# Cross-attention with neighbour features on one core: low-byte loads issued from ACT's queue, projection evicted by ACT and masked by POOL, layer statistics one step later

## The reference

```
for layer in (L0, L1):            # x -> x
    x = norm(attn(ctx, ctx, ctx) + x)   # per channel over tokens
x = x + neighbour_sum(ctx, x)     # L2
x = norm(attn(ctx, ctx, ctx) + x) # L3

attn: q, k, v = W_in @ ctx + b_in; 8 heads of 16, chunks of 64 tokens
      p = softmax(q k^T / 4 + (0 if mask > 0 else -1e9)); o = p v
      out = (W_out @ o + b_out) * mask
neighbour_sum: for each token its 30 nearest by channels 0..2 of ctx (top_k of
      -|p_i - p_j|^2); spherical features of the differences (rho, theta, phi);
      three 1x1 layers with batch norm over all batches; softmax over the 30;
      weighted sum of x at the neighbours
```

## Time and profile before

| what | us |
|---|---|
| three runs | 6677.32, 6666.21, 6669.81 |
| median | 6669.81 |
| the profiled execution: its time, its span | 6667.89, 6665.9 |
| busy in the span: PE, DVE, ACT, POOL | 5685.7, 5886.1, 4461.5, 3249.3 |
| mean granted clock of PE in the span | 0.904 of full |

### The profile page before, as it was taken

One profiled execution on the slowest core, in us unless ns is written; L12 is line 12 of the kernel. 1 busy time (PEld: TensorE's weight loads), 2 busy tenths in 40 slices (PEclk: granted clock), 3 DMA queues, 4 the chain that ended last, 5 costly groups with the idle time before them and its releaser, 6 DMA issues. The chain is left out here.

```text
span 6665.9 us, 228315 instructions
## 1 busy us (share of the span) xinstructions
PE 5685.7 (85%) x83284; PEld 3456.0 (52%) x83284; DVE 5886.1 (88%) x8332; ACT 4461.5 (67%) x17049; POOL 3249.3 (49%) x3279
## 2 busy tenths in 40 slices
PE   7888888888888888888888888888839949999998
PEld 3454545455555545545554555555423337677776
DVE  7999999999999999999999999999946588777776
ACT  7787878787787878787877878788822533333333
POOL 3455655555555555555655555555550023333332
PEclk9999988898888999898898998998859979999999
DMA  2333333233333333333233333333241013333332
GB/s 48 89 97 85 93 91 91 84 91 87 100 92 91 97 85 94 91 90 91 85 92 102 91 91 92 93 91 90 80 118 35 0 38 90 90 83 89 87 84 78
DMA packets 633780, 564.50 MB, mean 85 GB/s; under 512 B 535517, under 2 KB 557277, under 8 KB 598653
## 3 DMA queue, kind: packets, MB, share of 16 engines
q1 hardware_dynamic: 632572, 548.75, 29.1%
HBM read 380.55 MB, written 67.24 MB: 67 GB/s over the span
## 5 line engine op out<-in xcount | busy, mean ns | idle before, releaser
L703 ACT ACTIVATE prob<-SC,row_max 128x64 f32<-128x64 f32 x6144 | 1835.3, 327 | 671.7 <-DVE row_max L1032 664.8
L817 POOL TENSOR_TENSOR prob<-prob,row_rec 128x512 f32<-128x512 f32 x768 | 829.9, 1081 | 1897.7 <-DVE row_rec L1040 1897.1
L703 ACT ACTIVATION_READ_ACCUMULATOR prob<-SC,row_max 128x1 f32 x6144 | 1349.0, 220 | 0.0
L1024 DVE FIND_INDEX8 nbr<-top,dist 128x8 uint16<-128x1024 f32 x1024 | 1235.8, 1220 | 0.0
L1017 DVE MAX8 top<-dist 128x8 f32<-128x1024 f32 x1024 | 1194.1, 1207 | 12.6 <-DVE y_b L1055 10.3
L610 PE MATMUL PT<-ident,prob 128*128 128x128 f32 x3072 | 516.1, 295 | 573.9 <-ACT prob_t L710 563.2
L610 PEld LDWEIGHTS PT<-ident,prob 128*128 128x128 f32 x3072 | 383.6, 151 | 1076.8 <-issue 1033.2
L589 PE MATMUL SC<-k_bd,q_t 128*64 128x256 f32 x6144 | 935.8, 430 | 0.0
L1019 DVE MATCH_REPLACE8 dist<-top,dist 128x1024 f32<-128x1024 f32 x768 | 925.2, 1210 | 0.0
L1816 DVE TENSOR_TENSOR d_oh_a<-lo,iota_a 128x4096 bf16<-128x4096 bf16 x256 | 584.4, 2293 | 255.2 <-PE DM L1667 254.8
L1708 ACT ACTIVATE dense<-DM 128x512 f32<-128x512 f32 x512 | 305.6, 597 | 746.3 <-PE DM L1667 746.1
(11 more groups left out here) (194 smaller groups left out, 9538.6 us busy)
## 6 DMA issues: line engine op xcount, KB each, us to landing
low_all<-low_scratch SPq DMA_DIRECT2D x256, 1024.0 KB, 4.9
k_bd<-k_t SPq DMA_DIRECT2D x3072, 16.0 KB, 1.9
placed<-compact SPq DMA_DIRECT2D x256, 192.0 KB, 3.7
ctx<-in_ctx SPq DMA_DIRECT2D x32, 512.0 KB, 4.0
mask<-in_mask SPq DMA_DIRECT2D x32, 512.0 KB, 7.8
xb<-in_x SPq DMA_DIRECT2D x32, 512.0 KB, 4.3
x_scratch<-xb SPq DMA_DIRECT2D x32, 512.0 KB, 4.7
y_scratch<-y_b SPq DMA_DIRECT2D x32, 512.0 KB, 6.6
```

Of the source, the lines that this page charges most:

```text
L703: last = act.activation(prob[:, s % 4, g * CHUNK:(g + 1) * CHUNK], SC[:, s % 2, g * CHUNK:(g + 1) * CHUNK], ACT.Exp, bias=row_max[:, s % 2 ...
L817: pool.tensor_tensor(pr, pr, row_rec[:, r % 2, :].unsqueeze(2).to_broadcast([128, 8, CHUNK]), ALU.mult).then_inc(normed, 1)
L1024: last = dve.max_index(nbr[:, uu % BPB, t, k * 8:(k + 1) * 8], best, row)
```

## The change

1. LAG_BN and LAG_LN are one step larger: 8 and 9.
2. load_low moves from SP to ACT. ACT issues it at the end of its step, behind the exponentials and the copies of that step; tile 0 in step 24 + 6, tile 1 in step 24 + 8, tile t + 2 in step 24 + 12 + 3t. It waits for the stores of the low part (before SP waited for them once) and for the fetch as before.
3. The y bank is evicted by ACT with the bias added, in the same step, behind the other projections of that step and ahead of the copy to dist and the exponentials; ACT also takes over the three waits that guard y_b.
4. POOL multiplies y_b with the mask in place, for all three layers, once ACT has freed the bank, and signals y_masked; its addition of x waits for that. SP's store of the third layer waits for y_masked instead of masked, and for mask_row_ready ahead of the next mask load.

```diff
-LAG_BN, LAG_LN, LAG_TOP = 7, 8, 2
+LAG_BN, LAG_LN, LAG_TOP = 8, 9, 2
...
@@ sync, step
-                v = lagging(i, s, LOW_IN_AT)
-                if v is not None:
-                    sp.wait_ge(low_out, START + (i * BPB + v + 1) * 64)
-                    alone(sp)
-                    for t in range(2):
-                        load_low(i, v, t)
                 v = lagging(i, s, 6)
                 if v is not None:
                     b = i * BPB + v
-                    sp.wait_ge(masked, START + b + 1)
+                    sp.wait_ge(y_masked, START + (b + 1) * 2 * LAYERS)
+                    alone(sp)
+                    sp.wait_ge(mask_row_ready, START + b + 1)
...
-                at = lagging_tile(i, s, SELECT_AT)
-                if at is not None and at[1] + 2 < NT:
-                    load_low(i, at[0], at[1] + 2)
@@ scalar
+            def load_low(i, v, t):
+                tile = (i * BPB + v) * NT + t
+                act.wait_ge(low_out, START + (i * BPB + v + 1) * 64)
+                act.wait_ge(fetched, at_least(i, START + 2 * (tile - 1), START))
+                alone(act)
+                act.dma_start(low_all[:, t % 2, :], dram["low"][i * BPB + v][t:t + 1].broadcast_to([128, GROUPS * 128])).then_inc(low_in[t % 2], 16)
@@ scalar, step, behind the projections
+                r = s - LAG_Y
+                if real(i, r, STEPS) and r % 4 == 3:
+                    jj, uu = place(r)
+                    h = (r % PAIRS) // 4
+                    bank, free = produced(i, ("y", r // PAIRS, h))
+                    if h == 0:
+                        if jj == 0:
+                            act.wait_ge(applied[1], START + i * BPB + uu)
+                        elif jj == 1:
+                            act.wait_ge(y3_out, START + (i * BPB + uu) * 16)
+                        else:
+                            act.wait_ge(applied[0], START + i * BPB + uu + 1)
+                    act.activation(y_b[:, y_half(r // PAIRS), h * HALF:(h + 1) * HALF], bank, ACT.Identity, bias=b_out[:, jj:jj + 1]).then_inc(free, 1)
@@ scalar, step, behind the copy to picked
+                for t in range(2):
+                    v = lagging(i, s, LOW_IN_AT + 2 * t)
+                    if v is not None:
+                        load_low(i, v, t)
+                at = lagging_tile(i, s, SELECT_AT)
+                if at is not None and at[1] + 2 < NT:
+                    load_low(i, at[0], at[1] + 2)
@@ gpsimd, step
-                if real(i, r, STEPS) and r % 4 == 3 and place(r)[0] < 2:
+                if real(i, r, STEPS) and r % 4 == 3:
                     jj, uu = place(r)
                     h = (r % PAIRS) // 4
+                    half = slice(h * HALF, (h + 1) * HALF)
+                    mine = y_b[:, y_half(r // PAIRS), half]
                     copied(pool, i, ("y", r // PAIRS, h))
-                    half = slice(h * HALF, (h + 1) * HALF)
+                    landed(pool, mask_in, i, uu)
+                    pool.tensor_tensor(mine, mine, mask[:, uu % BPB, half], ALU.mult).then_inc(y_masked, 1)
+                if real(i, r, STEPS) and r % 4 == 3 and place(r)[0] < 2:
...
+                    pool.wait_ge(y_masked, START + (i * BPB + uu) * 2 * LAYERS + 2 * jj + h + 1)
@@ vector, step
-                r = s - LAG_Y
-                if real(i, r, STEPS) and r % 4 == 3:
...
-                    dve.wait_ge(pj_ready, START + use_count(i, use, 1))
...
-                    dve.scalar_tensor_tensor(y_b[:, y_half(r // PAIRS), half], PJ[:, use_parity(i, use), :], b_out[:, jj:jj + 1], mask[:, uu % BPB, half],
-                                             ALU.add, ALU.mult).then_inc(pj_free[use_parity(i, use)], 1)
...
```

More of the change, by code:

```diff
@@ L266, in attention_and_neighbours @@
         o_ready = sem("o_ready")
-        masked = sem("masked")
+        y_masked = sem("y_masked")
         added = sem("added")
@@ L498, in step @@
                         sp.dma_start(dram["sph"][1 + c][b], sph[:, c, :]).then_inc(sph_out, 16)
[L500 to L506, removed]
             all_steps(sp, step)
@@ L1040, in step @@
                     dve.reciprocal(row_rec[:, r % 2, :], row_sum[:, r % 2, :]).then_inc(recip_ready, 1)
-                r = s - LAG_Y
-                if real(i, r, STEPS) and r % 4 == 3:
-                    jj, uu = place(r)
-                    h = (r % PAIRS) // 4
-                    use = ("y", r // PAIRS, h)
-                    dve.wait_ge(pj_ready, START + use_count(i, use, 1))
[L1047 to L1054, removed]
-                    dve.scalar_tensor_tensor(y_b[:, y_half(r // PAIRS), half], PJ[:, use_parity(i, use), :], b_out[:, jj:jj + 1], mask[:, uu % BPB, half],
-                                             ALU.add, ALU.mult).then_inc(pj_free[use_parity(i, use)], 1)
[L1057 to L1060, removed]
                 r = s - LAG_BN
```

## The result

| | before | changed |
|---|---|---|
| median of the runs, us | 6668.76 | 6440.25 |
| all runs | 6666.21 to 6677.32 | 6437.35 to 6445.75 |
| span of the profiled execution, us | 6665.9 | 6436.4 |

The ratio is 0.9656, 95% interval 0.9639 to 0.9673: 228.5 us or 3.4% faster. The forecast was 6445.

What follows compares the result with a forecast made beforehand. DVE was taken to bound the attention stage. From 6667.89 us, 127 + 110 + 46 = 283 off and 16 + 42 = 58 back, 225 net, gave 6443, stated as 6445 us; range 6380 to 6555.

Steps and rivals of the forecast that it cites:

- Which engine bounds: Attention stage: DVE, 95% busy, sets the pace; time off its stream comes off the kernel's time if the others keep up.
- The broadcast: DVE's wait for the low-byte load of tile 6, issued late by SP, goes: 110 us gained.
- Rival A: The broadcast stall stays or moves, loads running beside the key copies: 6555 us, or 6500 for half; chance 0.13.
- The statistics: DVE's wait for POOL's residual addition ahead of the layer statistics goes with the later step: 46 us gained.
- The eviction: 192 projection evictions leave DVE's stream, with the searches' wait behind them: 127 us off, 58 back on.
- 16 us for late exponentials: ACT's arctangent-table step fails DVE in some batches, 0.5 us each: 16 us given back.
- The tight step: ACT's step with the arctangent table: exponentials end 1.5 us before DVE wants the sums; 0.3 us left after the change.
- PE's term: DVE's waits for PE's scores grow by 1.3 us per batch, bounds 0 and 3: 42 us given back.
- POOL's 244 us: 192 mask multiplications on POOL at 1.27 us each, on an engine busy 58% of the steady stretch.
- ACT's issues: 256 load issues taken at 0.4 us each in ACT's stream: 100 us, against about 860 us idle.
- Rival C: ACT held by its DMA issues, up to 5.73 us each during SP's key copies: slower, about 7250 us; chance 0.05.
- Rival B: Coupling: PE, POOL and ACT in tight steps stall DVE 4 to 5 us per batch; 140 us back, 6527; chance 0.11.

Runs made afterwards that it cites:

- e5: The changed kernel with the y eviction back on DVE; larger lags and loads on ACT's queue stay: 6503.45 us.
- e2: The kernel before with only the low-byte loads moved from SP to ACT's queue: 6556.95 us.
- e4: The kernel before with the loads of tiles 2 to 7 still on SP, ahead of their step's key copies, context load and x store: 6560.57 us.
- e1: The kernel before with only LAG_BN and LAG_LN one larger: 6622.24 us.
- e8: The changed kernel with two feature activations moved from ahead of the arctangent to behind the exponentials of the next two steps: 6413.41 us.
- S: The part of the change with the larger lags; alone on the kernel before: 6622.24 us.
- B: The part of the change with the low-byte loads (broadcasts) on ACT; alone on the kernel before: 6556.95 us.
- E: The part of the change with the eviction on ACT and the mask on POOL; alone on the kernel before: 6704.25 us.
- e3: The kernel before with only the eviction moved to ACT and the mask to POOL; small lags, loads on SP: 6704.25 us.
- e11: The changed kernel with the small lags back; eviction on ACT and loads on ACT's queue stay: 6549.53 us.
- e7: The changed kernel with every low-byte load issued as four DMAs of 32 partitions, 768 issues more on ACT: 6444.61 us.

## Why the prediction was right

**Which engine bounds.** Right. The two waits that were removed alone came off the time at their price or a little more and added up (e5), and the eviction came off less what DVE's other waits grew by.

**The broadcast.** Forecast 110 us; the wait fell by 106, and e2 alone gained 117. The reason given, SP's order, was shown by e4. Rival A is out: landings in the stretch were 4.2 to 8.2 us, median 5.1, much as before.

**The statistics.** Forecast 46; the row is gone, e1 gained 52.

**The eviction.** Forecast 127 off and 58 back, 69 net. Measured beside the other two parts, 63. The sum is right, its terms less so. The 16 us for late exponentials were put down as DVE waiting for ACT; that wait rose by 1 us. The tight step was the right one, but its lateness reached DVE by way of PE's scores two steps later, as e8 shows, so it belongs to PE's term: 42 forecast, 50 measured (94.0 - 43.7; 47 in the steady stretch), 10 of which e5 has without the eviction. And 16 us of longer one-hots (346.6 - 330.4) were in no term: I had read the hold between DVE and POOL from neither engine's rows. That the total came within 5 us is partly luck. The 42 was picked between bounds of 0 and 3 us per batch, which is 0 to 96 us, and the term that missed (16 for exponentials) was replaced by one of the same size that nobody had foreseen. Nor do the rows close: 127 + 106 + 46 = 279 us off and 67 back are 212, and the medians differ by 228.5. The time behind the last row maximum is 9 us shorter (1818 against 1827); the rest is in no row that I compared, and PE's granted clock rose from 0.90 to 0.92 in the stretch, which no run holds fixed.

**The order of the parts.** The prediction added the parts as if each had a worth of its own. For S and B that is so. For E it isn't, and no rival said it: without the larger lag and the earlier loads the same move costs 30 us. Where the prediction says that POOL's 244 us lie on an engine busy 58% of the stretch, the step "has one DVE step (at least 4 us) more" was carrying the whole gain: without it the statistics waited 135 and 136 us (e3, e11).

**ACT's issues.** The step took 0.4 us of ACT's stream for each. An issue row has 0.344 us, and next to none of it is taken from the activations (0.7 of 88.5 us). Rival C, the slower case, is out: its price was the length of SP's burst, and no issue on ACT took more than 0.394 us in the whole span, 0.369 in the stretch. The rule named beside it (the Trainium skill, Perfetto Trace Analysis, "DMA Instruction — HWDGE (DVE, Sync)"), by which ACT waits for one issue of SP at most, agrees with the changed kernel, where not even that is seen: the median is 0.345 us for issues that ran beside one of SP's and 0.344 for the others. In e7, with four in a row, 226 of 1024 took over 0.45 us, 214 of them beside an issue of SP, and all but ten stayed below the 0.7 us that the prediction allowed. Five took 1.4 to 1.7 us, two of these with no issue of SP beside them; the rule doesn't give those, and their cause stays open.

**Rival B** was right in kind (the new waits do come from the tight steps) and twice too large: 67 us came back by the rows (50 for scores, 16 in one-hots, 1 for sums) and 283 - 228.5 = 54 by the time, not 140.

Of the marks set beforehand: 144.6 us per batch against "some 145"; ACT's wait for maxima 411.5 us against "toward 400"; DVE's wait for scores in the stretch threefold, against "doubles or trebles". From the first statistics of the batch norms of L2 on (DVE's first st, 4982 us before, 4757 now) the rest took 1680 us, 4 less than before, where the prediction had no change.

## What to carry to other kernels

Before moving work from the bounding engine to an idle one, look at what the bounding engine waits for from that one: the added work lands in that wait first, and here only a larger lag (or an earlier load) turned the move into a gain. A late load needs its place in the issuing queue looked at before its transfer; ahead of eight small copies on the same queue it was as good as on a queue of its own. Test parts alone and in pairs: here one part was worth minus 30 or plus 63 us by its company.

## What the runs showed of the hardware

An issue on ACT (0.344 us of its queue) took next to no time from the activations, as its queue runs ahead of the engine: 87.8 of 88.5 us passed while an activation ran. With four in a row ACT stood idle for 53 us in e7, up to 2.3 at a time, and the 681 more issues in the steady stretch still left the kernel's time within the interval. A DVE tensor_scalar on bfloat16 (1.27 us) and a POOL instruction hold each other up, in both directions: 1.90 us for the one, 1.05 instead of 0.19 for the other; a tensor_scalar that began inside a tensor_tensor of POOL ended 1.08 us after that did. And a tensor_scalar on 3 partitions by 1024 elements, with compare and multiply and bfloat16 out, takes 3.70 us on POOL and 0.75 on DVE, where a tensor_tensor of 128 by 512 takes POOL 1.27.
